# Four heads' attention output divided on chip, and batch 1's norm and fp4 rounding moved forward, in a two-layer kernel

## The reference, cut to what matters

```python
x = L0_attn_x                                       # (2, 1024, 128), f32
x = x + _L0_attn_ref(_layernorm(x), Wq, bq, ...)    # 16 heads of 8, rotary
x = x + _L0_ffn_ref(_layernorm(x), w_gate, w_up, w_down)   # SwiGLU, hidden 352
x = x + _L1_attn_ref(_layernorm(x), log_A, B_w, ...)       # scan over time, 32 states
x = x + _L1_ffn_ref(_layernorm(x), gate_w, w1, ...)        # 8 experts, top 2

# in attention
attn = softmax(einsum('bhqd,bhkd->bhqk', q, k) * scale)
out = einsum('bhqk,bhkd->bhqd', attn, v)
return out.transpose(0, 2, 1, 3).reshape(b, t, d) @ Wo.T + bo

# every product of the SwiGLU layer
def fp4_linear(x, w):    # blocks of 16: scale = max|.|/6, round to the fp4 grid
    return jnp.einsum('bsk,nk->bsn', fp4_quant_dequant(x), fp4_quant_dequant(w))
```

## Time and profile before

| | |
|---|---|
| median of 3 runs | 950.13 us (949.09 to 950.76) |
| profiled execution | 949.47 us, of which the span is 947.7 us |
| TensorE busy | 794.8 us (84%) |
| VectorE busy | 788.2 us (83%) |
| ScalarE busy | 680.6 us (72%) |
| GpSimd busy | 238.7 us (25%) |
| chain that ended last | TensorE 58%, VectorE 17%, ScalarE 16%, issue 6% |

### The profile page before, as it was taken

One profiled execution on the slowest core, in us unless ns is written; L12 is line 12 of the kernel. 1 busy time (PEld: TensorE's weight loads), 2 busy tenths in 40 slices (PEclk: granted clock), 3 DMA queues, 4 the chain that ended last, 5 costly groups with the idle time before them and its releaser, 6 DMA issues.

```text
span 947.7 us, 12535 instructions
## 1 busy us (share of the span) xinstructions
PE 794.8 (84%) x4272; PEld 419.4 (44%) x4272; DVE 788.2 (83%) x746; ACT 680.6 (72%) x1300; POOL 238.7 (25%) x133
## 2 busy tenths in 40 slices
PE   5689999999999999985575774766667876999998
PEld 3312222212222222223543553655666765888886
DVE  5998898878888988885868989999989764787864
ACT  2407777767777777784455796999996756888884
POOL 3800000000000000010100357897977411222200
PEclk9859999989999999998688788999998998999999
DMA  4313223230123110002101144455544202211111
GB/s 130 100 31 98 77 75 101 67 103 17 43 71 101 35 37 12 13 12 61 45 0 32 63 163 151 159 200 177 180 170 143 91 0 98 82 67 67 44 45 45
DMA packets 41688, 75.97 MB, mean 80 GB/s; under 512 B 7584, under 2 KB 25352, under 8 KB 40856
## 3 DMA queue, kind: packets, MB, share of 16 engines
q1 hardware_dynamic: 41624, 75.17, 24.8%
HBM read 64.99 MB, written 8.85 MB: 78 GB/s over the span
## 4 chain that ended last, share of the span: by engine, by line
PE 58%; DVE 17%; ACT 16%; issue 6%; DMA 2%; POOL 1%; ACTq 0%; DVEq 0%; POOLq 0%; SPq 0%
PE ps L1570 14%; PE ps L1591 13%; ACT dtb L1008 8%; PE ps L1541 7%; PE ps L1843 6%; PE ps L1844 6%; PE ps L1845 6%; ACT abar L982 4%; DVE nmax L1175 2%; DVE hst L1310 2%; ACT prob L884 1%; PE ps L1644 1%; PE ps L1743 1%; PE ps L1530 1%; PE ps L1718 1%
## 5 line engine op out<-in xcount | busy, mean ns | idle before, releaser
L884 ACT ACTIVATE prob<-ps 128x512 f32<-128x512 f32 x512 | 264.4, 607 | 98.8 <-PE ps L1570 96.3
L1178 DVE TENSOR_REDUCE nmax_k<-ps 128x2 f32<-128x1024 f32 x224 | 262.4, 1220 | 37.9 <-PE ps L1541 36.7
L1570 PE MATMUL ps<-qs,ks 96*128 96x512 bf16 x512 | 163.2, 391 | 5.6 <-ACT prob L884 4.1
L811 POOL TENSOR_TENSOR hc<-hst,cbr 128x1024 f32<-128x1024 f32 x63 | 153.0, 2452 | 42.4 <-DVE hst L1310 23.8
L1310 DVE TENSOR_TENSOR_SCAN hst<-abar,ps 128x1024 f32<-128x1024 f32 x64 | 143.1, 2274 | 6.6 <-PE ps L1743 4.2
L1591 PE MATMUL ps<-prob,vq 128*16 128x512 f32 x1024 | 134.2, 601 | 0.8 <-ACT prob L884 0.7
L1420 DVE TENSOR_TENSOR act_l<-act_t,act_h 128x1024 fp32r<-128x1024 f32 x64 | 86.4, 1362 | 39.1 <-ACT act_h L1106 39.1
L1570 PEld LDWEIGHTS ps<-qs,ks 96*128 96x128 bf16 x512 | 40.2, 97 | 164.6 <-ACT prob L884 109.7
L1008 ACT ACTIVATE dtb<-dtxt,bt 128x128 f32<-128x128 f32 x352 | 107.5, 398 | 0.9 <-PE ps L1743 0.9
L1743 PE MATMUL ps<-ident,dtb 128*128 128x128 f32 x352 | 56.3, 303 | 57.2 <-DVE hst L1310 43.0
L1102 ACT ACTIVATE act_t<-ps,b1t 128x512 f32<-128x512 f32 x128 | 81.8, 681 | 31.3 <-PE ps L1845 31.3
(11 more groups left out here) (204 smaller groups left out, 1118.5 us busy)
## 6 DMA issues: line engine op xcount, KB each, us to landing
cbr<-s_dram SPq DMA_DIRECT2D x64, 512.0 KB, 4.0
gate<-c_dram SPq DMA_DIRECT2D x6, 1024.0 KB, 4.7
qs<-q_dram SPq DMA_DIRECT2D x16, 288.0 KB
ks<-k_dram SPq DMA_DIRECT2D x48, 96.0 KB
o_dram<-o_sb SPq DMA_DIRECT2D x16, 256.0 KB, 2.1
wf<-in_L_ffn_w SPq DMA_DIRECT2D x8, 256.0 KB, 5.1
wfq<-in_L_ffn_w SPq DMA_DIRECT2D x8, 256.0 KB, 5.3
gate<-c_dram SPq DMA_DIRECT2D x4, 512.0 KB, 4.3
```

The source lines that it names most:

```text
L811: nc.gpsimd.tensor_tensor(hc[:, m % RING], hst[:, m % RING], cbr[:, m % RING], ALU.mult).then_inc(s_hc, 1)
L884: nc.scalar.activation(prob[:, n % 8], ps[:, 4 + (first + n) % 3], ACT.Exp, scale=ATT_SCALE).then_inc(s_exp, 1)
L1178: nc.vector.tensor_reduce(nmax_k[:, half, kk, 2 * pair:2 * pair + 2, qt], ps[:, 2 * pair:2 * pair + 2, :], AX.X, ALU.max, negate=True).the ...
L1570: nc.tensor.matmul(ps[:, 4 + (first + n) % 3], ks[p][:, kt // 4, j, kt % 4 * P:(kt % 4 + 1) * P], qs[p][:, half, j, :], start=True, stop=T ...
```

## The change

It changes where the last four heads are divided, and the order of the SwiGLU layer.

- **Pass 7** is neither stored nor loaded back. VectorE turns each half of its `o_sb` in blocks of 32x32, so that numerators and denominator of a token lie in one partition, inverts, multiplies and turns it back (`divide_late`). `project_out(1)` multiplies 96 rows of `num` with the first 96 rows of Wo, and adds a second product of `late` (all 128 partitions) with `wo_late`, which holds Wo's last 32 rows at the partitions of `late` and zeros elsewhere. Four small DMAs fill `wo_late` in pass 3.
- **Passes 4 to 6** are loaded in pass 7 (`load_stored`), and the reciprocal of their denominators stands between the bias add and the residual adds of batch 0.
- **The turn of the rounded batch 0** and its copies go in front of the last pass's last products and its last evacuation.
- **TensorE** projects batch 1's output between gate/up 0 and 1, and turns the second hidden piece behind gate/up 4 to 7. **VectorE** takes batch 1's output and norm between hidden products 0 and 1 and rounds batch 1's normed input (piece 3) in front of hidden piece 1 (piece 4). ScalarE does batch 1's norm ahead of the first hidden copies. `down(1)` and the scan layer's first norm go into the rounding of piece 5, the B and C additions and softplus behind piece 6.

```diff
+        late = v[:].rearrange("p a k c -> p (a k c)")
-        X_PIECE = (1, 4)
-        HID_PIECE = (2, 3, 5, 6)
+        X_PIECE = (1, 3)
+        HID_PIECE = (2, 4, 5, 6)
...
+                sp.wait_ge(s_wt, 3)
+                for j in range(QUAD):
+                    sp.dma_start(wo_late[32 * j:32 * j + HD], wt[STORED[1].stop + HD * j:STORED[1].stop + HD * (j + 1), 5, :]).then_inc(s_wo, 16)
...
-                          4: lambda: load_out(0), 5: lambda: load_denominators(0)}.get(it))
-            load_out(1)
-            load_denominators(1)
+                          4: lambda: load_out(0), 5: lambda: load_denominators(0), 7: load_stored}.get(it))
...
+                if STEPS in between:
+                    between[STEPS]()
                 evacuate(it, 1)
...
-            turned_x(0, 0)
-            turned_x(1, 1)
+                STEPS: turned_first_x})
             for p in range(4):
                 evacuated(p)
-            turned_hidden(0)
             spread_act(1, 1)
             scale_act(1, 1)
-            turned_hidden(1)
+            turned_hidden(0)
             turned_x(2, 4)
             turned_x(3, 5)
+            for p in range(4, PAIRS):
+                evacuated(p)
+            turned_hidden(1)
...
+            spread_act(2, 0)
+            turned_hidden(2)
+            scale_act(2, 0)
...
+            def divide_late(half):
+
+                turned = late[:, SEQ + half * BANK:SEQ + (half + 1) * BANK]
+                cells = turned.rearrange("p (n r) -> p n r", r=32)
+                dve.wait_ge(s_vq, PASSES)
+                dve.wait_ge(s_o, 2 * PASSES + half)
+                dve_step(nc.vector.transpose(turned, o_sb[:, half, :]))
+                dve_step(nc.vector.reciprocal(cells[:, :, HD], cells[:, :, HD]))
+                dve_step(nc.vector.tensor_tensor(cells[:, :, 0:HD], cells[:, :, 0:HD], bc(cells[:, :, HD], HD), ALU.mult))
+                nc.vector.transpose(late[:, half * BANK:(half + 1) * BANK], turned).then_inc(s_late, 1)
...
+            divide(0)
+            add_bias(0)
+            inverse_denominators(1)
             attention_out(0)
...
+            divide(1)
+            add_bias(1)
+            divide_late(0)
...
-            hidden(0, scaled=lambda: inverse_denominators(1))
-            attention_out(1)
-            dve.wait_ge(s_res, 4)
-            norm_dve_mean(1, 1)
-            hidden(1)
-            down(0)
-            quant(4, x_half(xc, 1), x_half(sq, 1), (s_normed, 4))
-            down(1)
-            dve.wait_ge(s_res, 6)
-            norm_dve_mean(2, 0)
+            def second_batch_in():
+                divide_late(1)
+                attention_out(1)
+                dve.wait_ge(s_res, 4)
+                norm_dve_mean(1, 1)
+
+            def first_batch_out():
+                down(1)
+                dve.wait_ge(s_res, 6)
+                norm_dve_mean(2, 0)
+
+            hidden(0, halfway=second_batch_in)
+            quant(X_PIECE[1], x_half(xc, 1), x_half(sq, 1), (s_normed, 4))
+            hidden(1, multiplied=lambda: down(0))
...
-            hidden(2, free=(s_ht_ps, 3), before_last=lambda: bc_projected(0))
-            hidden(3, free=(s_ht_ps, 6), reduced=lambda: softplus_u(0), scaled=lambda: bc_projected(1), before_last=lambda: down(2))
+            hidden(2, free=(s_ht_ps, 3), scaled=first_batch_out)
+            hidden(3, free=(s_ht_ps, 6), scaled=lambda: down(2))
+            bc_projected(0)
+            bc_projected(1)
+            softplus_u(0)
...
+                    if b:
+                        pe.wait_ge(s_late, g % 2 + 1)
...
-            for p in range(4):
-                gate_up(p)
+            gate_up(0)
             project_out(1)
-            pe.wait_ge(s_res, 4)
+            gate_up(1)
+            gate_up(2)
+            gate_up(3)
             turn_hidden(0)
             down(0)
-            turn_hidden(1)
-            down(1)
             pe.wait_ge(s_quant, X_PIECE[1] + 1)
             turn_x(2, 4)
             turn_x(3, 5)
             for p in range(4, PAIRS):
                 gate_up(p)
+            turn_hidden(1)
+            down(1)
...
+            turn_hidden(2)
+            down(2)
             pe.wait_ge(s_dtw, 2)
             turn_pe(2, 0)
             turn_pe(2, 1)
             project(0)
             project(1)
-            turn_hidden(2)
-            down(2)
             turn_hidden(3)
             down(3)
```

More of the change, by code:

```diff
@@ L263, in build_kernel @@
         s_rden = sem("s_rden")
+        s_wo = sem("s_wo")
+        s_late = sem("s_late")
         s_ready = sem("s_ready")
@@ L651, in one_pass @@
                         load_heads(it + 2, (p + 2) % SETS, f)
-                store_out(it, 0)
+                if more:
+                    store_out(it, 0)
                 if more:
@@ L656, in one_pass @@
                     meanwhile()
-                store_out(it, 1)
+                if more:
+                    store_out(it, 1)
                 if again is not None:
@@ L662, in load_out, with load_stored @@
             def load_out(b):
[L664 to L668, removed]
+                sp.wait_ge(s_o_out[0], 16 * (4 * b + 4 - b + 1))
+                sp.wait_ge(s_o_out[1], 16 * (4 * b + 4 - b + 1))
+                rows = o_dram[4 * b:4 * b + 4 - b].rearrange("q (h r) t -> (q h) r t", r=32)
+                sp.dma_start(den[STORED[b], b], rows[:, HD]).then_inc(s_od[b], 16)
+                sp.dma_start(num[STORED[b], b * SEQ:(b + 1) * SEQ], rows[:, 0:HD]).then_inc(s_num, 16)
             def load_denominators(b):
                 sp.wait_ge(s_rden, b + 1)
-                sp.dma_start(r_dram[b].rearrange("h (c t) -> (h c) t", c=P // HEADS), den[:, b]).then_inc(s_od[b], 16)
+                heads = STORED[b].stop // HD
+                sp.dma_start(r_dram[b, 0:heads].rearrange("h (c t) -> (h c) t", c=P // HEADS), den[STORED[b], b]).then_inc(s_od[b], 16)
                 sp.wait_ge(s_od[b], 32)
-                sp.dma_start(rden[:, b], r_dram[b].unsqueeze(1).to_broadcast([HEADS, HD, SEQ])).then_inc(s_num, 16)
+                sp.dma_start(rden[STORED[b], b], r_dram[b, 0:heads].unsqueeze(1).to_broadcast([heads, HD, SEQ])).then_inc(s_num, 16)
                 sp.wait_ge(s_num, 32 * (b + 1))
                 sp.sem_inc(s_ready, 1)
+            def load_stored():
+                load_out(1)
+                load_denominators(1)
             def second_load():
@@ L912, in turned_x, with turned_first_x @@
                 nc.scalar.activation(xt[:, g * BANK:(g + 1) * BANK], ps[:, bank, :], ACT.Copy).then_inc(s_xt, 1)
+            def turned_first_x():
+                turned_x(0, 0)
+                turned_x(1, 1)
             def turned_hidden(g):
@@ L1010, in scaled @@
                         ins.then_inc(s_dtb, 1)
[L1012 to L1017, removed]
             act.wait_ge(s_dtw_ps, 1)
@@ L1200, in inverse_denominators, with add_bias, divide, attention_out @@
                 dve.wait_ge(s_od[b], 16)
-                nc.vector.reciprocal(den[:, b], den[:, b]).then_inc(s_rden, 1)
-            def attention_out(b):
+                nc.vector.reciprocal(den[STORED[b], b], den[STORED[b], b]).then_inc(s_rden, 1)
+            def add_bias(b):
+                for g in (2 * b, 2 * b + 1):
+                    ins = nc.vector.tensor_tensor(x[:, 4 * g:4 * g + 4, :], x[:, 4 * g:4 * g + 4, :],
+                                                  bo_all[:].unsqueeze(1).to_broadcast([P, 4, D]), ALU.add)
+                dve_step(ins)
+            def divide(b):
                 w = slice(b * SEQ, (b + 1) * SEQ)
                 dve.wait_ge(s_ready, b + 1)
-                nc.vector.tensor_tensor(num[:, w], num[:, w], rden[:, b], ALU.mult).then_inc(s_att, 1)
+                nc.vector.tensor_tensor(num[STORED[b], w], num[STORED[b], w], rden[STORED[b], b], ALU.mult).then_inc(s_att, 1)
+            def divide_late(half):
[7 more added lines that the diff above has]
+                nc.vector.transpose(late[:, half * BANK:(half + 1) * BANK], turned).then_inc(s_late, 1)
+            def attention_out(b):
                 for g in (2 * b, 2 * b + 1):
-                    dve_step(nc.vector.tensor_tensor(x[:, 4 * g:4 * g + 4, :], x[:, 4 * g:4 * g + 4, :],
-                                                     bo_all[:].unsqueeze(1).to_broadcast([P, 4, D]), ALU.add))
                     dve.wait_ge(s_y, g + 1)
@@ L1224, in _, with hidden @@
             quant(1, x_half(xc, 0), x_half(sq, 0), (s_normed, 3))
-            def hidden(g, halfway=None, **order):
+            divide(1)
+            add_bias(1)
+            divide_late(0)
+            def hidden(g, halfway=None, multiplied=None, **order):
                 for m in range(2):
```

19 lines of the change are left out of this document (13 added, 6 removed).

## The result

| | before | after |
|---|---|---|
| median | 950.97 us (11 runs, 948.9 to 955.58) | 947.87 us (11 runs, 945.11 to 949.76) |
| ratio | | 0.9968, 95% interval 0.9954 to 0.9982 |
| profiled execution | 949.47, span 947.7 | 945.11, span 943.3 |

The kernel is 3.1 us faster, where 4.9 were forecast, and the interval of the ratio leaves out 1.

What follows compares the result with a forecast made beforehand. VectorE's waits between the last attention pass and first scan (18.4 and 4.4 us) were the gain to be had. Walked gain 8.6, taken as 7.5, less 2.9 is 4.6, taken as 4.9: median 945.2 us, range 942.2 to 949.0.

Steps and rivals of the forecast that it cites:

- the walk: Both orders followed engine by engine from last attention pass to first scan; centring at 521.6 instead of 530.2, 8.6 us gained.
- The new wait in the pass: Last attention pass: VectorE waits 2.6 us for den before the reciprocal; batch 0 and the pass's end 2.9 us late.
- Rival A: Last pass absorbs the new wait through reserves of score tiles; the 2.9 us are not lost, 942.3 us; chance 0.13.
- The late division: Pass 7's on-chip division: two transposes of 0.65 us, reciprocal 0.2, product 0.3; 1.9 us a half, bounds 0.9 and 3.2.
- The first part of the walk: SwiGLU: hidden product 0 ends at 434.3, adds and mean 440.4, hidden product 1 442.3, its rounding 452.5.
- the norm 9.7 us later: Batch 1's norm ends at 455.9, 9.7 us after ScalarE's last copy at 446.2; VectorE waits 3.4 us.
- The down product of group 1 ends at 481.4, just in time.: SwiGLU, after gate/up 4 to 7 (465.4 to 475.0): ready before VectorE needs it at 482.3.
- rival C: Gate/up 4 to 7 run at half clock, delaying group 1's down product: 9 us lost, 954 us; chance 0.06.
- it decides from some 1 us of delay on: Half-clock gate/up 4 to 7 cost time from about 1 us of delay, since slack before group 1's down add is 0.9.
- C's price: Half-clock gate/up pairs taken at up to 4.33 us instead of 2.4, ending at 482.7 instead of 475.0.
- The rest: Later SwiGLU and projections: 2.0 us wait for a down product starting at half clock; B/C projections behind it; centring at 521.6.
- walks that come out early: Walking the order before came out 1.0 to 1.5 us early, so the stage's 8.6 us gain was taken as 7.5.

Runs made afterwards that it cites:

- e1: Changed kernel with the reciprocal of batch 1's denominators moved between the roundings of the weights and of batch 0: 942.89 us, ratio 0.9928 to the kernel before.
- e3: Changed kernel with VectorE waiting for GpSimd's power of batch 1's norm before the last two passes of hidden piece 0's rounding: 942.75 us, ratio 0.9923.
- e2: Changed kernel with 20 overwritten products added on TensorE in four gaps (6, 4, 7 and 3): 942.48 us, ratio 0.9923 to the kernel before.
- e8: Changed kernel with reciprocal later and VectorE waiting for GpSimd's power, no added products: 940.67 us, ratio 0.9890 to the kernel before.
- e6: Changed kernel with its on-chip division and reciprocal kept, but engine orders of the kernel before restored: 953.15 us, ratio 1.0029 to the kernel before.
- e4: Changed kernel with reciprocal later, VectorE waiting for the power, and TensorE kept busy (7, 3, 7 and 3 products): 939.11 us, ratio 0.9884.
- e9: Changed kernel with reciprocal later, VectorE waiting for the power, and 8 and 3 products added before turn_hidden(2) and down(3): 936.11 us, ratio 0.9847.

## Why the prediction was right, and where its sizes were off

The mechanism held: the order removed the large waits, the new wait in the pass went through to its end, and the sum came out in the right direction. It was 1.8 us too high, mainly by two terms of the walk that were too small. In absolute time the median is 947.87, not 945.2; 0.8 of these 2.7 us are the kernel before, which measured 950.97 beside the changed one instead of 950.13.

For comparison I subtract the earlier start and the pass's 2.8 us: a time after, less 1.74, is in the walk's clock.

- **The new wait in the pass.** Forecast 2.6 us of wait and 2.9 of delay, at the end of the pass too; measured 2.83 and 2.8. e1 shows that it is a real loss: without it the pass is about 3 us shorter. Rival A falls.
- **The late division.** 1.9 us a half forecast; measured 428.81 to 430.89, 2.1 us. A 128x512 f32 turn took 0.71 us, 0.65 were forecast. The reason given, that the f32 passes of this stage all go by the element, was too wide: before, a `tensor_scalar` over 1024 f32 elements (L1264) took 0.69 us, as long as an add of 512. My estimate of 1.24 us from the Trainium skill's "VectorE: DVE Perf Modes" (The three transpose paths), doesn't hold for f32 at this size. Its "Vector Engine (DVE) Microarchitecture Reference" (3.8 The reshape front-end and per-opcode configuration) says that a 32x32 turn sustains one element a cycle and lane; the trace agrees: a turn of 512 elements at 0.71 us is as long as the add of 512 elements in the earlier trace rows, 0.69.
- **The first part of the walk** held to 0.2 us at each step: hidden product 0 ends at 434.1 (434.3), the adds and mean at 440.4 (440.4), hidden product 1 at 442.3 (442.3), its rounding at 452.5 (452.5).
- **The step that failed: "the norm 9.7 us later".** ScalarE's last copy ended on time (446.1 to 446.2), but scaling ended at 457.5 instead of 455.9. I had carried over the 3.5 us of waiting for GpSimd from the earlier trace rows; it was 5.13. In the new order GpSimd's two instructions are held for longer by the passes of VectorE that run at that moment. Mis-sized by 1.6 us; e3 shows the cause, and the last section has the rows.
- **"The down product of group 1 ends at 481.4, just in time."** Gate/up 4 to 7 were taken at 9.6 us and took 12.56, partly at the half clock: VectorE waited 1.70 us. That is rival C in small; I had its mechanism, and "it decides from some 1 us of delay on", but put it in the range instead of the sum. e2 and e8 show it: with the full clock 9.73 us and 0.49 us of wait or none. C's price was read a little low: the pair of 4.33 us ran in a stretch granted 0.62, and a pair at 0.50 took 5.06 us in e6.
- **The rest** (down product 2 at half clock, 2.0 forecast, 2.44 measured; 0.6 at the projections) held. The four DMAs in pass 3 took 0.68 us each in SyncE's queue, not 0.43; nothing shows that it cost anything, as pass 4's first evacuation came 1.07 us sooner, like the rest of the attention. Centring came at 524.4 against 521.6 in the walk. The three overruns of 1.6, 1.7 and 0.4 us are 3.7; the pieces between them took some 1.0 us less than walked, which was luck. I had taken off 1.1 us for walks that come out early; 2.8 were due. So the stage's gain was 5.9, not 7.5, less 2.8: 3.05 us, and the medians say 3.1. The 0.3 us that the forecast put on top of its sum, from 4.6 to 4.9, did not come either.

## What to carry to other kernels

Walk the new order through engine by engine with the durations of the old trace; but a duration is only good with its company: look at what the neighbour that shares a path with it does in the new order, and at what TensorE did just before. A wait placed on purpose on the engine that would be idle anyway (VectorE, 2.4 us) can free another (GpSimd) and win time. Put a load that an engine must wait for ahead of work that nobody needs yet, not ahead of the chain that sets the pass.

## What the runs showed of the hardware

**VectorE holds GpSimd off.** The passes of VectorE that ran beside batch 1's power, first in the changed kernel, then before with GpSimd's rows:

```profile
450.95 1.62 DVE L512 SCALAR_TENSOR_TENSOR fx<-fe,fx 128x1408 f32<-128x1408 f32 x1
452.61 1.62 DVE L517 TENSOR_TENSOR hid_q<-fx,fblk 128x1408 f32<-128x1408 f32 x1
```

```profile
461.21 1.62 DVE L502 SCALAR_TENSOR_TENSOR fx<-hid,fblk 128x1408 f32<-128x1408 f32 x1
462.87 0.90 DVE L505 TENSOR_SCALAR fe<-fx 128x1408 int32<-128x1408 int32 x1
462.17 0.73 POOL L452 TENSOR_SCALAR stat<-stat 128x8 f32<-128x8 f32 x1 [47.72 <-ACT sq L432]
462.98 2.29 POOL L453 TENSOR_TENSOR stat<-stat,expo 128x8 f32<-128x8 f32 x1
```

In the changed kernel the pass over `fe` and `fx` ended at 452.57 and GpSimd's 0.2 us instruction, begun at 451.00, at 452.63. VectorE's next pass ended at 454.23 and the power, begun at 452.71, at 455.73, which is 1.5 us later, about its own length of 1.64. Before, it was the same with less left to wait for: the instruction ended at 462.90, 0.07 us after the pass, and the power at 465.27, again 1.5 us after the pass that ran when it began, which there reads only one tensor in the engines' common memory (SBUF) and takes 0.90 us. That is the 1.6 us between 5.13 and 3.50. Each GpSimd instruction waits for the VectorE instruction that is running, not for those behind it. Not every instruction of VectorE does it: beside a scan of 2.28 us, which reads one tensor in SBUF and one in PSUM (the memory that TensorE writes to), GpSimd's two took 0.20 and 1.64 us in the changed kernel (529.58 and 529.86). It goes the other way round too. In the scan layer a product of GpSimd over 1024 elements runs from 561.25 to 563.62 (2.37 us), and VectorE's L1326, begun at 561.62, takes 3.08 us, to 564.70, where the same pass took 1.23 us at 517.39. The Trainium skill, "SBUF — State Buffer", SBUF: two separate sides, says that the two engines share a port pair as an exclusive lock, held for the whole instruction by whoever comes first, and names VectorE instructions with two SBUF inputs; the rows here agree with it. Read beforehand beside the walk, it could have given the 1.6 us.

**The place of a rise or fall of TensorE's clock repeats, and moves with the order.** The same third down product took 4.68 and 4.67 us in the two profiles of the changed kernel and 2.94 in e1, which differs only in where the reciprocal stands in the pass. By the stage, 20 added products gave 4.2 us on the changed kernel (e2) and 0.5 on e8 (e4), while 11 gave 3.5 on e8 (e9). So the gain of keeping TensorE busy isn't a property of a gap alone. Where the clock was full anyway, as at gate/up 4 to 7 on e8, the three products added ahead of it only held it up. So it has to be tried in the final order.
